# High halves of the first image on GpSimd, and a reworked chain between the Gram stage and the first convolution, in a two-layer normalise-and-convolve kernel

## The reference, cut to what matters

```python
def _gn(v, G=8, eps=1e-5):            # group norm, 8 groups of 2 channels
    ...
x = x + _L0_conv_ref(_gn(x), ...)     # x: (8, 16, 512, 512) float32
x = x + _L1_conv_ref(_gn(x), L1_conv_weight)
```

## Time and profile before

| | us |
|---|---|
| median of 3 runs (lowest, highest) | 1730.44 (1728.99, 1730.54) |
| the profiled execution's own time | 1728.56 |
| its span | 1726.8 |
| PE busy | 1630.3 (94%) |
| DVE busy | 1294.9 (75%) |
| ACT busy | 1144.3 (66%) |
| POOL busy | 112.0 (6%) |
| granted TensorE clock, mean | 0.990 |

### The profile page before, as it was taken

How to read it: one execution, slowest core, us unless ns; L and a number is a source line. 1 busy time by engine, 2 the same in 40 slices (tenths; PEclk the granted TensorE clock), 3 DMA queues, 4 the chain that set the end, 5 groups by cost and what they waited for, 6 DMA issues and landing times.

```text
span 1726.8 us, 63815 instructions
## 1 busy us (share of the span) xinstructions
PE 1630.3 (94%) x28906; PEld 1260.8 (73%) x28906; DVE 1294.9 (75%) x1744; ACT 1144.3 (66%) x1029; POOL 112.0 (6%) x347
## 2 busy tenths in 40 slices
PE   5888888789899999999999999999999999999999
PEld 4787778655467777887688778867786778677766
DVE  5999899889977777777777777777777777777600
ACT  6888878589666666666666666666666666666444
POOL 0000000031100020002000200020002000100100
PEclk9999999989999999999999999999999999999999
DMA  9999999935466566666666666666666665665255
GB/s 386 421 421 422 422 422 421 379 92 161 119 199 211 201 198 211 210 201 198 213 207 201 198 212 208 200 199 211 210 200 198 209 212 185 213 206 204 112 203 203
DMA packets 99668, 409.99 MB, mean 237 GB/s; under 512 B 16883, under 2 KB 17384, under 8 KB 83048
## 3 DMA queue, kind: packets, MB, share of 16 engines
q1 hardware_dynamic: 98025, 405.94, 65.7%
q0 software_dynamic: 672, 0.08, 0.1%
q10 hardware_dynamic: 735, 0.37, 0.1%
HBM read 271.83 MB, written 134.50 MB: 235 GB/s over the span
## 4 chain that ended last, share of the span: by engine, by line
PE 75%; DVE 12%; issue 7%; ACT 4%; DMA 2%; DVEq 0%; ACTq 0%; SPq 0%; POOL 0%; POOLq 0%
PE ps L527 72%; DVE x L810 9%; ACT x L633 2%; DMA x<-x_pix 1%; ACT x L668 1%; ACT x L670 1%; DMA x<-wf 1%; DVE x L1013 1%; DVE x L864 1%; DVE stats L1030 1%; PE ps L452 1%; PE ps L453 0%; ACT x L674 0%; PE ps L456 0%; PE ps L463 0%
## 5 line engine op out<-in xcount | busy, mean ns | idle before, releaser
L527 PE MATMUL ps<-x,wc 64*64 64x512 f16 x24540 | 1339.9, 377 | 10.3 <-DVE x L1013 9.4
L527 PEld LDWEIGHTS ps<-x,wc 64*64 64x64 f16 x24540 | 992.7, 107 | 351.5 <-issue 21.4
L864 DVE SCALAR_TENSOR_TENSOR x<-xin,gnp,x 128x1028 f16<-128x1028 f32 x247 | 320.3, 1298 | 234.6 <-ACT x L633 234.5
L633 ACT ACTIVATE x<-xin,gnp 128x1028 f16<-128x1028 f32 x247 | 286.4, 1160 | 307.6 <-PE ps L527 302.4
L684 ACT ACTIVATE outb<-ps,bias 128x1024 f32<-128x1024 f32 x256 | 285.3, 1114 | 155.0 <-PE ps L527 155.0
L1013 DVE SCALAR_TENSOR_TENSOR x<-ps,gnp,x 128x1024 f16<-128x1024 f32 x256 | 325.1, 1270 | 24.3 <-ACT x L670 24.0
L452 PE MATMUL ps<-x 128*128 128x129 f16 x2048 | 254.1, 224 | 59.0 <-DVE x L810 58.6
L810 DVE SCALAR_TENSOR_TENSOR x<-x 128x2048 bf16<-128x2048 f32 x128 | 282.8, 2283 | 19.3 <-DMA x<-wf 17.4
L1030 DVE BATCH_NORM_STATS2 stats<-ps 128x6 f32<-128x512 f32 x440 | 283.6, 687 | 11.1 <-ACT x L674 8.5
L619 ACT ACTIVATE x<-x 128x2048 f16<-128x2048 f32 x128 | 240.1, 1908 | 52.6 <-PE ps L453 36.0
L452 PEld LDWEIGHTS ps<-x 128*128 128x128 f16 x2048 | 197.7, 98 | 78.6 <-DVE x L810 78.6
(11 more groups left out here) (144 smaller groups left out, 292.2 us busy)
## 6 DMA issues: line engine op xcount, KB each, us to landing
x<-x_pix SPq DMA_DIRECT2D x128, 1024.0 KB, 11.5
out<-outb SPq DMA_DIRECT2D x256, 512.0 KB, 3.7
xin<-x_tiles SPq DMA_DIRECT2D x239, 514.0 KB, 3.6
xin<-x_tiles SPq DMA_DIRECT2D x8, 642.5 KB, 4.1
x<-x_tiles SPq DMA_DIRECT2D x9, 514.0 KB, 7.2
w<-taps_scratch SPq DMA_DIRECT2D x60, 8.0 KB, 2.7
w<-taps_scratch SPq DMA_DIRECT2D x30, 16.0 KB, 3.1
taps_scratch<-x POOLq DMA_DIRECT2D x21, 3.0 KB, 1.8
```

The source lines that it names most:

```text
L527: return nc.tensor.matmul(to.rearrange("p (r w) -> p r w", w=NCOL), lhs, two, start=first, stop=last)
L633: nc.scalar.activation(planes[:, 0, a:a + w], x_at(g), ACT.Identity, scale=gnp[:, 1, b:b + 1]).then_inc(hi0_ready, 1)
L864: V.scalar_tensor_tensor(planes[:, 1, a:a + w], x_at(g), gnp[:, 1, b:b + 1], planes[:, 0, a:a + w], ALU.mult, ALU.subtract).then_inc(lo0_r ...
```

## The change

By its parts:

- `hi0` of chunks 13 to 31 goes from ScalarE to GpSimd (`first_hi0`: a tensor_scalar by `gnp`, 128x1028 f32 to f16), behind that chunk's `first_pad`. ScalarE does all statistics of chunks 0 to 28 of image 0 (`by_act`), so VectorE's bn_stats of every fourth chunk go.
- GpSimd's 21 tap stores go to SyncE, three in each of the steps 1 to 7.
- Gram stage: TensorE takes a block's 16 hi*hi products as soon as `ahi` is there and the 16 lo*hi ones after `alo`; opening and closing matmuls are f16; images 0 to 3, 4 and 5, 6, and 7 are folded apart, each part waiting for one mask at a time; sums and diagonal of images 0 to 6 run ahead of the last image's end.
- Chain: the first half of `gnp` has a matmul and a signal of its own (`Z_SCALE`, `Z_GNP`), ahead of the projection's; a table that holds tanh and the sine is loaded ahead of the tanh; `load_weights` has 8 transfers, not 12; the part of `weights0` that needs no loaded weights runs first; `hi0(4)` runs ahead of ScalarE's weight loads; `tsum` is made after the weights are handed over, and `shift_of` runs at job 1.

```diff
--- before.py
+++ after.py
-        return n < TAIL0 and n % 4 != 3
+        return n < TAIL0
...
+def by_pool(g):
+
+    return HI_FIRST <= g < NCH
+
+
+def hi0_count(g):
+
+    return g + 1 if g < HI_FIRST else g + 1 - (NCH - HI_FIRST)
+
+
+def spot_before(g):
+
+    return g - (LAP if g < LAP + NSEVEN else NSEVEN if g < TURN + NX else NX)
...
+        zeroh = zerof[:, :].bitcast(F16)
...
-                g = (half * 2 + r) * 2 * C
-                for row, count, m in ((r, 4, 0),) if half == 0 else ((2 + r, 2, 0), (r, 2, 128)):
-                    for ci in range(2):
-                        at_ = g + ci * C
-                        eng.dma_start(w32[at_:at_ + C, m:m + 64 * count].rearrange("c (a m) -> c a m", m=64),
-                                      taps[b, :, row:row + count, ci:ci + 4, :].rearrange("c a q o -> c a (q o)")
-                                      ).then_inc(signal, 16)
+                for ci in range(2):
+                    at_ = ((half * 2 + r) * 2 + ci) * C
+                    eng.dma_start(w32[at_:at_ + C, :].rearrange("c (a m) -> c a m", m=64),
+                                  taps[b, :, r:r + 4, ci:ci + 4, :].rearrange("c a q o -> c a (q o)")
+                                  ).then_inc(signal, 16)
...
+                if 0 < g < B:
+                    taps_out(sp, g, taps_rest)
...
-            def gram_pair(bb):
+            def gram_pair(bb, last=False):
 
                 for h in range(2):
                     b = bb * 2 + h
                     accs = [ps[:, 2 * part + h, 0:P + 1] for part in range(2)]
                     pe.wait_ge(a_mask, 4 * b + 4)
                     for acc in accs:
-                        nc.tensor.matmul(acc, zerof[:, 0:P], zerof[:, 0:P + 1], start=True, stop=False)
+                        nc.tensor.matmul(acc, zeroh[:, 0:P], zeroh[:, 0:P + 1], start=True, stop=False)
                     with pe.Fori(0, NACH // ASLOTS) as jj:
                         for s in range(ASLOTS):
-                            pe.wait_ge(a_lo, b * NACH + jj * ASLOTS + s + 1 + ASLOTS)
+                            k = b * NACH + jj * ASLOTS + s
+                            pe.wait_ge(a_hi, k + 1)
                             for q in range(ABLK):
-                                rhs = ahi[:, s % AROUND, q, 0:P + 1]
-                                nc.tensor.matmul(accs[0], ahi[:, s % AROUND, q, 0:P], rhs, start=False, stop=False)
-                                mm = nc.tensor.matmul(accs[1], alo[:, s % AROUND, q, :], rhs, start=False, stop=False)
+                                nc.tensor.matmul(accs[0], ahi[:, s % AROUND, q, 0:P], ahi[:, s % AROUND, q, 0:P + 1],
+                                                 start=False, stop=False)
+                            pe.wait_ge(a_lo, k + 1 + ASLOTS)
+                            for q in range(ABLK):
+                                mm = nc.tensor.matmul(accs[1], alo[:, s % AROUND, q, :], ahi[:, s % AROUND, q, 0:P + 1],
+                                                      start=False, stop=False)
                             mm.then_inc(a_gram, 1)
                     for acc in accs:
-                        mm = nc.tensor.matmul(acc, zerof[:, 0:P], zerof[:, 0:P + 1], start=False, stop=True)
+                        mm = nc.tensor.matmul(acc, zeroh[:, 0:P], zeroh[:, 0:P + 1], start=False, stop=True)
                     mm.then_inc(zpe, 1)
-
-            def fold(h):
-
-                pe.wait_ge(a_mask, 4 * (4 * h + 4 + 2))
+                    if last and h == 0:
+                        fold(B - 2, B - 1)
...
+            def fold(lo, hi):
+
                 for f, name in enumerate(("fold", "fold2")):
-                    m = nc.tensor.matmul(ps[0:C, 6 + h, 0:512], c(name),
-                                         gmask[:, f, 4 * h:4 * h + 4, :].rearrange("p b q -> p (b q)"),
+                    pe.wait_ge(a_mask, 8 + 4 * (hi - 1) + f + 1)
+                    m = nc.tensor.matmul(ps[0:C, 6 + lo // 4, P * (lo % 4):P * (lo % 4) + P * (hi - lo)], c(name),
+                                         gmask[:, f, lo:hi, :].rearrange("p b q -> p (b q)"),
...
-            fold(1)
+            fold(B - 1, B)
+            pe.wait_ge(a_mask, 8 + 4 * B)
...
+            pe.wait_ge(zve, Z_SCALE)
+            mm(ps[:, 3, 0:16], c("rep", C), zc[0:C, 320:336])
             pe.wait_ge(zve, Z_FORMS)
-            mm(ps[:, 5, 0:72], c("ones", C), zc[0:C, 96:168], False)
-            mm(ps[:, 5, 128:160], c("rep", C), zc[0:C, 320:352])
+            mm(ps[:, 5, 0:72], c("ones", C), zc[0:C, 96:168])
+            mm(ps[:, 2, 0:16], c("rep", C), zc[0:C, 336:352])
...
+                        if job == 1 and q == 0:
+                            pe.wait_ge(shift_x, 1)
+                            pe.wait_ge(shift_w, 1)
+                            shift_of(0, ps[:, 7, 0:1]).then_inc(shift_pe, 1)
...
+            nc.scalar.preload_act_table_set("silu_and_others")
...
-            for g in range(1, NX):
+            for g in range(1, NX + 1):
                 hi0(g)
             act.wait_ge(zdma, 16 * 4)
             load_weights(act, 0, ((0, 1), (1, 1)), w_in)
-            for g in range(NX, HI_FIRST):
+            for g in range(NX + 1, HI_FIRST):
                 hi0(g)
             for g in range(ALL + LAG):
                 early = g < ALL and g >= NCH and by_act(*divmod(g, NCH))
                 if early:
                     hi1(g)
-                if ahead_hi(g) is not None:
+                if ahead_hi(g) is not None and not by_pool(ahead_hi(g)):
...
+            def first_hi0(g):
+
+                a = nat_at(g)
+                w = loads(g)
+                pool.wait_ge(pe_done, JOB0[spot_before(g)] + 1)
+                G.tensor_scalar(planes[:, 0, a:a + w], x_at(g), gnp[:, 1, 0:1], None, ALU.mult).then_inc(pool_hi0, 1)
...
-            for g in range(LAP + NX):
+            for g in range(NCH):
                 first_pad(g)
-            pool.wait_ge(zve, Z_TAPS)
-            pool.wait_ge(zdma, 16 * 4)
-            for b in range(1, B):
-                taps_out(pool, b, taps_rest)
-            for turn in range(NCH):
-                if LAP + NX <= turn + 9 < NCH:
-                    first_pad(turn + 9)
-                if turn - 1 in ENDS:
-                    ends(0, turn - 1)
+                if by_pool(g):
+                    first_hi0(g)
+                if g - NSEVEN - 2 in ENDS:
+                    ends(0, g - NSEVEN - 2)
...
+                    if last and h == 1:
+                        fold_sums(B - 2, B - 1, 3).then_inc(zve, 1)
...
+            def diagonal(lo, hi):
+
+                squares = diag[:, lo:hi, :]
+                ve.wait_ge(zve, count[0])
+                go(V.tensor_tensor(squares, gram[:, lo:hi, :], c("id16", C).unsqueeze(1).to_broadcast([C, hi - lo, C]), ALU.mult))
+                ve.wait_ge(zve, count[0])
+                return go(V.tensor_reduce(zc[0:C, 8 + lo:8 + hi], squares, AX.X, ALU.add))
...
+            go(fold_sums(0, 4, 1))
+            go(fold_sums(4, B - 2, 2))
+            diagonal(0, B - 2)
             with ve.Fori(B // 2 - 1, B // 2) as bb:
-                halves_pair(bb)
+                halves_pair(bb, last=True)
...
-            n = go(fold_sums(1))
-            ve.wait_ge(folded, 3)
-            go(V.tensor_copy(zc[0:C, 0:8], ps[0:C, 4, 0:8]))
-            need(n)
-            diag = w32[0:C, 0:B * C].rearrange("p (b c) -> p b c", b=B)
-            link(V.tensor_tensor(diag, gram, c("id16", C).unsqueeze(1).to_broadcast([C, B, C]), ALU.mult))
-            at(link(V.tensor_reduce(zc[0:C, 8:16], diag, AX.X, ALU.add)), Z_MOM)
+            go(fold_sums(B - 1, B, 4))
+            diagonal(B - 2, B)
+            ve.wait_ge(folded, 5)
+            at(link(V.tensor_copy(zc[0:C, 0:8], ps[0:C, 4, 0:8])), Z_MOM)
...
+            at(go(V.tensor_scalar(scale0, irms, YS, None, ALU.mult)), Z_SCALE)
...
+            at(go(V.tensor_copy(gnp[:, 0:2, :], ps[:, 3, 0:16].rearrange("p (f b) -> p f b", f=2))), Z_GNP)
...
+            go(V.tensor_copy(gnp[:, 2:4, :], ps[:, 2, 0:16].rearrange("p (f b) -> p f b", f=2)))
...
                 if part == 0:
-                    ve.wait_ge(w_in, 16 * 12 * (b + 1))
-                    after(post(V.tensor_scalar(w32[:, :], w32[:, :], gnp[:, 3, b:b + 1], None, ALU.mult)))
+                    if b > 1:
+                        ve.wait_ge(l1_ready, b - 1)
+                    after(post(V.tensor_scalar(wtmp1[:, :], c("id0"), gnp[:, 2, b:b + 1], None, ALU.mult)))
                 elif part == 1:
-                    after(post(V.scalar_tensor_tensor(w32[:, :], c("id0"), gnp[:, 2, b:b + 1], w32[:, :],
+                    ve.wait_ge(w_in, 16 * 8 * (b + 1))
+                    after(post(V.scalar_tensor_tensor(w32[:, :], w32[:, :], gnp[:, 3, b:b + 1], wtmp1[:, :],
                                                       ALU.mult, ALU.add)))
                 elif part == 2:
-                    both_columns(tsum, w32).then_inc(shift_w, 1)
```

(12 more changed lines are left out.)

73 lines of the change are left out of this document (42 added, 31 removed).

## The result

| | before | the change |
|---|---|---|
| median of 8 runs each (lowest, highest), us | 1729.93 (1728.99, 1730.54) | 1735.27 (1733.64, 1736.39) |
| ratio, 95% interval | | 1.0031 [1.0021, 1.0041] |
| span of the profiled execution | 1726.8 | 1734.6 |
| last `alo` starts | 327.0 | 328.7 |
| from there to the first job | 32.2 | 26.6 |

The forecast was 1716.5 and "faster". The last four rows add up to the spans' difference of 7.8 us: 1.7 (the Gram stage, bound by its transfers, ended later in this execution), -5.7, +11.3, +0.5. The first is scatter (between the profiled executions of this study the last `alo` starts at 327.0 to 328.7), and the medians differ by 5.3. The chain came out as forecast; the first image's stage grew where it was to shrink.

What follows compares the result with a forecast made beforehand. Bounds: Gram stage by reading x, image 0 by ScalarE then VectorE, the steady part by TensorE. Chain 5.6 plus stage 8.9, less 0.5 for uneven fits, gives 14.0: 1714.6 profiled, 1716.5 as median; range 1711 to 1732.

Steps and rivals of the forecast that it cites:

- The chain: From the last Gram block to the first job: reordered, shorter work starts the first job 5.6 us earlier, at about 353.6.
- The stage without GpSimd's limit: Image 0, first job to means: TensorE sets the pace if GpSimd keeps up; 95.5 us against 104.4, gain 8.9.
- Rival 3: Image 0's stage stays bound by VectorE, at 2.39 of 2.56 us; only the chain's 5.6 is left: 1724.9, chance 0.11.
- The unknown: GpSimd's pass, T: Duration of GpSimd's hi0 pass over 1028 elements: bounds about 1.05 and 3.5 us, taken as 1.1, nearest to a contiguous copy.
- The upper bound: GpSimd's pass priced from strided f16 copies at 3.2 ns an element: T of 3.5 us, time 1749.5.
- The formula for T: Image 0: VectorE's step is 2.39 + (T + 0.3 - 1.2); loss is 15 x (T - 1.07) - 3 us if positive.
- Full exclusion: GpSimd and VectorE exclude each other, so hi0 and padding beyond lo1's 1.2 us delay the next lo0.
- Rival 2: GpSimd becomes the bound at lo0 of chunks 17 to 31, slower than before; 1733.5 at T 2.4, chance 0.13.
- its point of 2.2 us: The pass length T from which GpSimd as the bound decides, the loss having eaten the 14 us gain.

Runs made afterwards that it cites:

- e1: The change without its GpSimd part (hi0 back on ScalarE, every fourth chunk's statistics back on VectorE), chain rework kept: 1724.31 us, ratio 0.9966 to before.
- e5: The change with GpSimd's pass cut to 257 of 1028 columns on chunks 13 to 30, chunk 31 on ScalarE: 1716.97 us, ratio 0.9925 to before.
- e8: The change with single GpSimd passes probed behind its last work; on 1028 elements a copy took 1.04 us, tensor_scalar 2.8 to 2.9, two-input product 1.90.
- e13: The change with GpSimd's pass on chunks 13 to 31 as a cast, without the multiplication: 1718.81 us, ratio 0.9939 to before.
- e9: The change with GpSimd's pass written as a product with gnp repeated along the row, nothing left out: 1728.46 us, ratio 0.9992 to before.
- e3: The change with GpSimd's pass cut to a quarter of the columns for chunks 13 to 30, chunk 31 whole: 1719.69 us, ratio 0.9939 to before.
- e4: The change with only odd chunks 13 to 31 on GpSimd, the even ones on ScalarE: 1723.98 us, ratio 0.9966 to before.
- e11: The change with a second probe behind its last work: short VectorE operations during GpSimd passes; a cast of 1.04 us held VectorE for 1.07.

## Why the prediction was wrong, point by point

- **The chain: right.** Forecast 5.6 us, 5.7 by the rows, 5.7 by e1. Counted from the last `alo`'s start, the first job was forecast 26.6 us later (353.6 - 327.0) and came 26.6 later; `Z_S` 19.9 and 19.8. That `lo0(0)` is what ends last ahead of the first taps is in the rows: L1045 starts as it ends, and without a wait for the sines. The gathered weights were not late: VectorE's fourth `lo0` starts at 352.48, the last step of the weights at 354.59, and no wait is left between; TensorE's 1.47 us behind the warm-up are VectorE's own work.
- **The stage without GpSimd's limit: nearly right.** 95.5 forecast, 97.55 in e5, and TensorE did set the pace to 433 us there. Rival 3 is thereby worth 2 us and not 8.4.
- **"The unknown: GpSimd's pass, T": here it failed.** T was taken at 1.1 us, from a copy's 0.76 ns an element, as the row it was "nearest to" by its contiguous access and single input. It is 2.90. The copy's price was right for copies (1.04 by e8), and e13, which has that T, came within 2.3 us of the forecast. What was wrong is the choice of the likeness: in e8 what an element costs on GpSimd goes by the operation, and an operation with one contiguous input (2.86) costs more than one with two (1.90). The upper bound, 3.2 ns an element, was the near one.
- **The formula for T: that `lo0` and the pass add up was right, the count was not.** It gave a step of 2.39 + 2.9 + 0.3 - 1.2 = 4.39 us; 4.09 was measured, since the padding lies beside `lo0`. And it charged 15 chunks less 3 us, together 24.5 us at T = 2.90, where 18.1 were lost over e5: GpSimd's and TensorE's lead lasted to chunk 20 and through 18 jobs, and 12 chunks paid 1.53 each. For the product (1.90) it gave 9.5, and 12.0 were lost.
- **Full exclusion: wrong for this operation, right for others.** VectorE was held for the first 0.9 to 1.1 us of a pass, not for 2.9. It changed little for the change's own time: in the ring it is `lo0` that holds the pass, and `lo0` waits for the pass's result and not for a port.
- **Rival 2 is what happened**, "GpSimd becomes the bound", in the chunks it named (the last 12 of its 15), beyond its point of 2.2 us; at 2.90 its formula says 1741, 5.7 too high. It had 0.13. The Trainium skill (GPSIMD Engine Reference, Performance versus the Vector engine) has VectorE about twice as fast at elementwise work, which made T 2.4 and the time 1733.5. Against the measured 2.90 that is nearer than the forecast. That two inputs are its slow case and one-input operations are excepted agrees with e8 for a copy (1.04), and not for the operation of this change, where two inputs took 1.90 and one 2.86.

## What to carry to other kernels

A pass moved to an idle engine is priced by a row of the same operation on that engine; a row of another operation, however alike in shape, is no more than a bound, and where the bounds lie on both sides of the point at which the verdict turns, the chance of the bad side has to be near a half. Where two engines take turns (one needs the other's result and shuts it out while it uses it), add their durations and compare the sum with the bound engine's step: 1.2 + 2.9 against 2.56 settles this change in a line. Two reworks that come in one change should be timed apart: here a gain of 5.7 us was hidden under a loss of 10.8.

## What the runs showed of the hardware that was not expected

- GpSimd, 1028 elements a partition: copy or cast 1.04 us, tensor_tensor 1.90, tensor_scalar 2.83 to 2.91, whatever the types; a tensor_tensor with a repeated operand is the quicker way to write a multiplication (e9 is 6.8 us shorter than the change), though it holds VectorE throughout.
- How long GpSimd shuts VectorE out depends on the operation: all of a cast or a product, somewhat over a third of a tensor_scalar (0.63 of 1.64 us, 1.1 of 3.0). The Trainium skill (SBUF — State Buffer, Who interferes with whom) says, where it tells how VectorE's modes that use both port pairs contend with GpSimd, that who issues first has the shared pair for the whole instruction. GpSimd's tensor_scalar does not agree: VectorE's copy was held for 1.12 of 3.02 us. GpSimd's cast and products did hold VectorE's two-input products throughout (1.07 of 1.04, 1.94 of 1.90). That f32 copies and tensor_scalars of VectorE are held and reductions never are agrees with the same section: 1.12, 1.11 and 0.22 us at the longest.
- One thing stays open: the copy of 32x257 on VectorE that lasted 3.44 us beside a pass of 4.29 in e3, and 3.46 in e4. By e11 a copy is held for little over a third of such a pass, and that one was of 64 elements; no run here tells why the longer one was held to the end.
